# All scan drives on GpSimd, and the product placed behind both scans of the next pair

## The chip, the cores and the metric

The kernel runs on one core of one Trainium2 chip. The metric is the device time of one launch in microseconds (us): the median of 3 runs of the kernel before is 22461.38 us (22454.06 to 22490.8). The engines are called by the profile's names: PE (TensorE, matmuls), PEld (its weight loads), DVE (VectorE), ACT (ScalarE), POOL (GpSimd) and SP (SyncE, which issues most of the DMAs). Each engine runs its own list of instructions in order and waits on semaphores that the others raise.

## The reference, cut to what matters

The input is 64 samples of 96 channels by 28 x 28 pixels (784 pixels, in float32). Each sample passes through four layers; everything is computed per sample. The first layer is a convolution block (a 1x1 expansion to 576 channels, a 5x5 depthwise convolution with kernels mixed per sample, a squeeze gate, a 1x1 projection). The second is a group norm and a selective scan in four directions, the part that the change touches most:

```python
def step(h, inps):
    u_t, dt, B_t, C_t = inps
    dA = jnp.exp(dt[:, :, None] * A)
    h = dA * h + (dt * u_t)[:, :, None] * B_t[:, None, :]
    y = jnp.einsum('bdn,bn->bd', h, C_t) + Dv * u_t
    return (h, y)
```

It has 768 channels (4 directions of 192) with 16 states each, over 784 positions. The third layer mixes positions by a Fourier transform and adds a quantized two-layer network, the fourth is an attention without softmax (linear, so it folds into small matrices) and another such network.

## The kernel before

The 768 channels lie as six groups of 128 partitions. One **unit** is one group with one state index: 6 x 16 = 96 units per sample (`NU`), taken two by two as 48 **pairs** (`NP`, list `PAIRS`). A unit needs, in this order:

- a **decay**, exp(delta x A), 128x784, on ACT (`decaying`);
- a **drive**, (delta x u) x B, 128x784: in the even unit of a pair on DVE, in the odd one on POOL (`driving`, there are two functions of that name). The row of B comes broadcast to 128 partitions by DMA into one of four buffers `Bb`;
- a **scan** on DVE (`scanning`, the instruction TENSOR_TENSOR_SCAN): state = decay x state + drive along the 784 positions.

After both scans of a pair, PE sums halves of the partitions into PSUM (`state_sum`, the function `scan` of the tensor block: the "fold"). DVE multiplies that with C (`product`, into `prod`), and PE adds the products up in PSUM (`summation`, `scan_sum`).

The even unit's decay lies in PSUM (tile `decay_even`, one buffer), the odd unit's in SBUF (tile `decay`, two buffers). So the even scan reads one input from PSUM and one from SBUF, the odd scan reads both from SBUF. There are three state buffers and two drive buffers.

The scan of sample i is the backbone of a pass. Everything else is threaded between its units: the *tail* of sample i-1 (norm and gate behind the scan, `post`; the Fourier layer, `mixer`; the networks, `ffn`; `attention`), and the *head* of sample i+1 (the convolution layer, the group norm and the projections, `head` and `pre`). Each of these is a Python generator that yields a place on an axis counted in units (0 to 96); `go_on(between, 2 * p)` issues all steps whose place has come. The places are tables written out by hand: `CONV_SLOTS`, `HEAD`, `FAR`, `READ_AT`, `LOG_AT` and the numbers behind `yield`. They are the same for all engines, so a table sets the order on PE, ACT, DVE, POOL and SP at once. The loop (`Fori`) covers samples 1 to 62; samples 0 and 63 stand outside it.

For a DVE pair the order before is: drive of the even unit, even scan, product of the pair before, steps, odd scan, steps. POOL's list holds the odd drives, the twelve tiles of convolution weights per sample (`taps`) and one power (`gst`, reciprocal root of the group variance).

## Time and profile before

| | before |
|---|---|
| median of 3 runs | 22461.38 us |
| the profiled execution's own time | 22505.68 us |
| its span, first to last instruction | 22503.9 us |
| PE busy | 18818.0 us (84%) |
| DVE busy | 19251.1 us (86%) |
| ACT busy | 15624.5 us (69%) |
| POOL busy | 6356.1 us (28%) |
| mean granted TensorE clock | 0.894 |

Busy time is the sum of the time in which an engine executes instructions. Matmul ends are modelled, so a busy PE isn't a PE at its peak. Where a row gives "idle before" and a releaser, the engine stood still in front of that instruction until the one named had ended. An instruction that is held up after it has started shows no idle time: its own duration grows.

### The profile page before, as it was taken

Reading aid. Unit: us, or ns where it says so; the run is one execution under the profiler, and the core shown is the slowest. Engines: PE = TensorE matmul, PEld = TensorE weight load, DVE = VectorE, ACT = ScalarE, POOL = GpSimd, SP = SyncE. Lnnn points to the kernel's source line nnn. Section 1 sums busy time; section 2 is a strip of 40 time slices with the busy share of each in tenths; the row PEclk is TensorE's granted clock in tenths of the full one; section 3 lists DMA queues with packets and bytes.
Section 4 is the critical chain, followed back from the end, with each engine's and each line's share of the span. In section 5 each row is a group of like instructions: output and inputs, shape, how many; then the busy total and the mean of one; then the engine's idle time right before and its main releaser. Section 6 shows DMA issues by size and latency. Waiting matters only on the chain.

```text
span 22503.9 us, 334261 instructions
## 1 busy us (share of the span) xinstructions
PE 18818.0 (84%) x100834; PEld 6890.1 (31%) x100834; DVE 19251.1 (86%) x17938; ACT 15624.5 (69%) x21098; POOL 6356.1 (28%) x3909
## 2 busy tenths in 40 slices
PE   5888888888888888888888888888888888888887
PEld 1333333333333333333333333333333333333332
DVE  4888888888888888888888888888888888888887
ACT  3767777777677677776776777767767767777674
POOL 1222222222222222222222222222222222222222
PEclk8889898898898998988988889889889898898898
DMA  5555555555555555555555555545555555555552
GB/s 144 143 135 140 140 138 139 135 144 137 132 142 138 137 142 135 143 138 134 140 141 133 140 136 141 140 133 143 138 133 143 139 139 141 134 142 136 134 141 75
DMA packets 1418366, 3083.16 MB, mean 137 GB/s; under 512 B 207812, under 2 KB 786696, under 8 KB 1407859
## 3 DMA queue, kind: packets, MB, share of 16 engines
q1 hardware_dynamic: 1372146, 2992.85, 51.6%
q10 hardware_dynamic: 44032, 64.26, 1.1%
q8 instruction: 993, 16.27, 0.3%
q14 instruction: 1195, 9.78, 0.2%
HBM read 2796.25 MB, written 221.51 MB: 134 GB/s over the span
## 4 chain that ended last, share of the span: by engine, by line
issue 67%; POOL 15%; PE 8%; DVE 5%; ACT 4%; DMA 1%; POOLq 0%; ACTq 0%; SPq 0%; DVEq 0%
POOL drive L1576 13%; PE bank L575 3%; DVE state L1381 3%; PE state_sum L575 2%; PE pair L575 2%; POOL taps L1563 2%; ACT work L920 1%; DVE drive L1237 1%; PE scan_sum L575 1%; ACT L920 0%; ACT decay_even L920 0%; DVE work L1237 0%; ACT du L920 0%; DVE prod L1237 0%; ACT decay L920 0%
## 5 line engine op out<-in xcount | busy, mean ns | idle before, releaser
L1576 POOL TENSOR_TENSOR drive<-du,Bb 128x784 f32<-128x784 f32 x3072 | 5689.7, 1852 | 15638.6 <-DVE drive L1237 15638.6
L575 PE MATMUL state_sum<-state,fold 128*64 128x392 f32 x24576 | 5610.5, 585 | 1052.4 <-DVE state L1381 1029.9
L1381 DVE TENSOR_TENSOR_SCAN state<-decay_even,drive 128x784 f32<-128x784 f32 x3072 | 5500.2, 1790 | 128.4 <-ACT decay_even L920 17.6
L1381 DVE TENSOR_TENSOR_SCAN state<-decay,drive 128x784 f32<-128x784 f32 x3072 | 5473.3, 1782 | 0.2 <-POOL drive L1576 0.2
L920 ACT ACTIVATE decay_even<-delta,alog 128x784 f32<-128x784 f32 x3072 | 2821.6, 918 | 3240.8 <-DVE state L1381 3224.0
L1237 DVE TENSOR_TENSOR prod<-state_sum,Cb 128x784 f32<-128x784 f32 x3072 | 2950.6, 960 | 1906.4 <-PE state_sum L575 1902.4
L575 PE MATMUL scan_sum<-prod,fold 128*64 128x392 f32 x12288 | 2990.4, 568 | 1500.0 <-DVE prod L1237 1493.9
L575 PEld LDWEIGHTS state_sum<-state,fold 128*64 128x64 f32 x24576 | 1706.4, 154 | 4427.8 <-issue 2288.4
L575 PE MATMUL bank<-rep,taps 120*32 120x392 f32 x30720 | 2973.9, 514 | 96.1 <-ACT image L920 33.8
L920 ACT ACTIVATE decay<-delta,alog 128x784 f32<-128x784 f32 x3072 | 2890.3, 941 | 115.6 <-issue 72.7
L1237 DVE TENSOR_TENSOR drive<-du,Bb 128x784 f32<-128x784 f32 x3072 | 2943.0, 958 | 18.9 <-DVE work L1237 11.9
L914 ACT ACT_TABLE_LOAD x1707 | 2190.1, 1283 | 400.8 <-issue 375.3
L920 ACT ACT_TABLE_LOAD x1648 | 2114.4, 1283 | 33.6 <-DVE mean L1253 1.8
L575 PEld LDWEIGHTS scan_sum<-prod,fold 128*64 128x64 f32 x12288 | 660.1, 144 | 3173.8 <-DVE prod L1237 2436.7
L575 PEld LDWEIGHTS bank<-rep,taps 120*32 120x32 f32 x30720 | 856.1, 111 | 2175.3 <-issue 2022.2
L920 ACT ACTIVATE dwo<-bank,bn 128x392 f32<-128x392 f32 x768 | 521.1, 679 | 1402.0 <-PE bank L575 1401.9
L920 ACT ACTIVATE work<-pair 96x392 f32<-96x392 f32 (+5 forms) x2560 | 1135.7, 483 | 441.6 <-PE pair L575 421.4
L575 PE MATMUL bank<-dwo,wdl 6*128 6x392 f32 x1536 | 759.0, 575 | 401.9 <-ACT du L920 275.9
L575 PE MATMUL bank<-rep,wt 96*32 96x392 f32 x4608 | 518.8, 590 | 239.8 <-ACT xc L920 235.1
L920 ACT ACTIVATE work<-work 96x392 f32<-96x392 f32 (+6 forms) x897 | 492.4, 594 | 243.2 <-DVE work L1237 240.0
L920 ACT ACTIVATE work<-work,ffn_b 128x392 f16<-128x392 f16 (+1 forms) x1024 | 636.7, 622 | 33.4
L575 PE MATMUL pair<-work,mean 96*96 96x392 f32 (+1 forms) x1536 | 616.2, 524 | 22.2 <-ACT work L920 22.1
(169 smaller groups left out, 17504.8 us busy)
## 6 DMA issues: line engine op xcount, KB each, us to landing
Bb<-bc_rows SPq DMA_DIRECT2D x3072, 392.0 KB, 4.4
rep<-expanded_images SPq DMA_DIRECT2D x3840, 168.0 KB
Cb<-bc_rows SPq DMA_DIRECT2D x3072, 196.0 KB, 3.6
expanded_images<-image SPq DMA_DIRECT2D x1152, 112.0 KB, 2.5
rep<-conv_in_images SPq DMA_DIRECT2D x1152, 112.0 KB, 3.9
dwo<-in_pww SPq DMA_DIRECT2D x65, 1152.0 KB, 7.3
conv_in_images<-image SPq DMA_DIRECT2D x384, 112.0 KB, 3.2
xc<-xc ACTq DMA_DIRECT2D x384, 98.0 KB, 2.6
```

The lines of the kernel that those rows point to most:

```text
L575: return pe.matmul(out, lhsT, rhs, start=start, stop=stop)
L914: act.preload_act_table_set(LOG_EXP)
L920: return act.activation(out, in_, f, bias=bias, scale=scale, **more)
L1237: return v.tensor_tensor(out, a, b, op)
L1381: v.tensor_tensor_scan(state[:, j % STATES, :], DP[:, 0:L] if j % 2 == 0 else decay[:, j // 2 % DECAYS, :], drive[:, j % 2, :], 0.0, ALU.m ...
L1563: pool.tensor_tensor(taps[:, t % 2, cols, :], values.unsqueeze(2).to_broadcast([KP, n, 32]), cmask[:, :].unsqueeze(1).to_broadcast([KP, n, ...
L1576: pool.tensor_tensor(drive[:, j % 2, :], du[:, 2 * s + r, :], Bb[:, b % BSLOTS, :], ALU.mult).then_inc(drive_r.sem, 1)
```

## The change

Five things change; the computation stays the same.

1. POOL computes all 96 drives of a sample, DVE none. A drive waits until the scan two units earlier has ended (its buffer is free then).
2. On DVE the order for a pair is now: even scan, steps, odd scan, product of the pair before, steps.
3. There are three decay buffers used in turn, unit j taking number j mod 3. Number 0 lies in PSUM (tile `decay_third`), the others in SBUF. So of six units in a row, units 0 and 3 have their decay in PSUM and units 1, 2, 4 and 5 in SBUF. ACT issues the decay of unit j two units ahead of the place where its other steps stand. State buffers go from three to four; the space comes from `seT2`, which now lies in free partitions of `wdl`.
4. On PE the fold of a pair stands ahead of the summation of the pair before; it was behind it.
5. Steps of head and tail stand at other places; the power of the group norm moves from POOL to ACT (as Ln and Exp), and the bias of the squeeze gate is added by a matmul on PE where DVE added it.

```diff
-DECAYS = 2
+DECAYS = 3
 PRODS = 2
-STATES = 3
+STATES = 4
...
-CONV_SLOTS = (1, 2, 3, 5, 7, 8, 9, 10, 11, 12, 13, 14, 15, 17, 18, 19, 20, 21, 23, 24, 26)
+CONV_SLOTS = (1, 2, 3, 4, 6, 7, 9, 10, 11, 13, 14, 15, 16, 17, 18, 19, 20, 21, 23, 24, 26)
...
+        def decay_of(j):
+
+            return decay[:, j % DECAYS - 1, :] if j % DECAYS else DP[:, 0:L]
...
             def scan(i, *between):
                 for p in range(NP):
-                    if p >= 1:
-                        summation(i, p - 1)
-                    elif later(i):
-                        summation(i - 1, NP - 1)
-                    go_on(between, 2 * p + 1)
                     pe.wait_ge(state_r.sem, state_r.at(i, 2 * p + 2))
...
                     last.then_inc(folded.sem, 1)
                     go_on(between, 2 * p + 2)
+                    if p >= 1:
+                        summation(i, p - 1)
+                    elif later(i):
+                        summation(i - 1, NP - 1)
+                    go_on(between, 2 * p + 3)
...
+                if j >= DECAYS or later(i):
+                    act.wait_ge(state_r.sem, state_r.at(i, j - DECAYS + 1))
+                ac(decay_of(j), delta[:, k, :], ACT.Exp, scale=alog[:, k, n:n + 1]).then_inc(decay_r.sem, 1)
...
                 for p in range(NP):
-                    driving(2 * p)
                     scanning(2 * p)
+                    go_on(between, 2 * p)
+                    scanning(2 * p + 1)
                     if p >= 1:
                         product(i, p - 1)
                     elif later(i):
                         product(i - 1, NP - 1)
-                    go_on(between, 2 * p)
-                    scanning(2 * p + 1)
                     go_on(between, 2 * p + 1)
...
-                yield 64.4
-                pool.wait_ge(g_rs.sem, g_rs.at(i))
-                pool.tensor_tensor(gst[:, 6:7], gst[:, 6:7], eps[0:C, 2:3], ALU.pow).then_inc(g_pw.sem, 1)
...
-                pool.wait_ge(drive_r.sem, drive_r.at(i, j))
+                if j >= 2 or later(i):
+                    pool.wait_ge(state_r.sem, state_r.at(i, j - 1))
                 pool.tensor_tensor(drive[:, j % 2, :], du[:, 2 * s + r, :], Bb[:, b % BSLOTS, :], ALU.mult).then_inc(drive_r.sem, 1)
 
             def scan(i, *between):
-                for j in range(1, NU, 2):
+                for j in range(NU):
                     driving(i, j)
```

What it makes of the order is shown at three places of the loop's pass. (SCALAR_TENSOR_TENSOR with the output `state` is the scan; REGISTER_ALU and ISA rows compute the counts that are waited for.)

DVE at the first layer norm of the mixer (`work<-work 96x784`), before:

```order
L1381 SCALAR_TENSOR_TENSOR state<-decay,drive 128x784 [waits drive_ready]
L1417 ISA
L1419 TENSOR_TENSOR work<-work 96x784 [waits norm_rstd]
L1368 REGISTER_ALU
L1237 TENSOR_TENSOR drive<-du,Bb 128x784 [waits state_ready,b_loaded0]
L1377 REGISTER_ALU
L1380 REGISTER_ALU [waits even_decay]
L1381 SCALAR_TENSOR_TENSOR state<-decay_even,drive 128x784 [waits drive_ready]
L1237 TENSOR_TENSOR prod<-state_sum,Cb 128x784 [waits summed,states_folded,c_loaded1]
```

and after the change:

```order
L1376 SCALAR_TENSOR_TENSOR state<-decay_third,drive 128x784 [waits drive_ready,decay_ready]
L1368 REGISTER_ALU [waits c_loaded1]
L1249 TENSOR_TENSOR prod<-state_sum,Cb 128x784 [waits summed,states_folded]
L1411 ISA
L1413 TENSOR_TENSOR work<-work 96x784 [waits norm_rstd]
L1374 REGISTER_ALU
L1376 SCALAR_TENSOR_TENSOR state<-decay,drive 128x784 [waits drive_ready,decay_ready]
```

The drive is gone from DVE's list, the product stands behind the second scan of a pair, and the norm's multiplication stands behind the product where it stood behind a scan.

POOL at the beginning of a pass, before (odd drives, and `taps` of the next sample's convolution):

```order
L1574 ISA [waits b_loaded1]
L1575 ISA [waits du_ready]
L1576 TENSOR_TENSOR drive<-du,Bb 128x784 [waits drive_ready]
L1574 REGISTER_ALU [waits b_loaded1]
L1575 REGISTER_ALU [waits du_ready]
L1576 TENSOR_TENSOR drive<-du,Bb 128x784 [waits drive_ready]
L1558 ISA
L1563 TENSOR_TENSOR taps<-kern,cmask 120x320 [waits bank_read]
```

and after:

```order
L1567 ISA [waits b_loaded0]
L1569 ISA [waits du_ready]
L1570 TENSOR_TENSOR drive<-du,Bb 128x784 [waits state_ready]
L1570 TENSOR_TENSOR drive<-du,Bb 128x784 [waits state_ready,du_ready,b_loaded1]
L1567 REGISTER_ALU [waits b_loaded0]
L1569 REGISTER_ALU [waits du_ready]
L1570 TENSOR_TENSOR drive<-du,Bb 128x784 [waits state_ready]
L1569 REGISTER_ALU [waits du_ready,b_loaded1]
L1570 TENSOR_TENSOR drive<-du,Bb 128x784 [waits state_ready]
L1554 ISA
L1559 TENSOR_TENSOR taps<-kern,cmask 120x320 [waits bank_read]
```

Two drives per pair stand in POOL's list now, and each waits for a scan (`state_ready`) where it waited for DVE's drive.

PE around the squeeze gate of the next sample (`bank<-zse`) and the last matmuls of the mixer (`w2T`), before:

```order
L575 MATMUL pair<-cosm,work 96x396 x2
L719 REGISTER_ALU
L575 MATMUL scan_sum<-prod,fold 64x392 x2
L638 REGISTER_ALU
L575 MATMUL bank<-zse,seT 128x1 x6
L699 REGISTER_ALU
L575 MATMUL state_sum<-state,fold 64x392 x4
L575 MATMUL pair<-work,w2T 96x392 x4
```

and after:

```order
L577 MATMUL state_sum<-state,fold 64x392 x4
L640 REGISTER_ALU
L577 MATMUL bank<-seb,ident 128x6
L577 MATMUL bank<-zse,wdl 128x1 x6
L577 MATMUL scan_sum<-prod,fold 64x392 x2
L577 MATMUL pair<-work,w2T 96x392 x4
```

The fold (`state_sum`) of a pair now precedes the summation (`scan_sum`) of the pair before, and one small matmul brings the gate's bias.

## Rows read from the trace of the kernel before

**Rows 1.** The page's span and busy times (engine, us, share, instructions)
```profile
span 22503.9 us, 334261 instructions
PE 18818.0 (84%) x100834; PEld 6890.1 (31%) x100834; DVE 19251.1 (86%) x17938; ACT 15624.5 (69%) x21098; POOL 6356.1 (28%) x3909
```
**Rows 2.** The scans by tile: duration ns min/median/max, first and last start
```profile
L1381 DVE TENSOR_TENSOR_SCAN state<-decay_even,drive x3072: 1790/1790/1793, 343.0 to 22363.5; 128x784 f32<-128x784 f32 x192
L1381 DVE TENSOR_TENSOR_SCAN state<-decay,drive x3072: 1775/1781/2028, 345.0 to 22366.1; 128x784 f32<-128x784 f32 x192
```
**Rows 3.** DVE groups by form (busy us, mean ns, idle before, releaser)
```profile
L1237 DVE TENSOR_TENSOR prod<-state_sum,Cb 128x784 f32<-128x784 f32 x3072 | 2950.6, 960 | 1906.4 <-PE state_sum L575 1902.4 <-issue 0.8
L1237 DVE TENSOR_TENSOR drive<-du,Bb 128x784 f32<-128x784 f32 x3072 | 2943.0, 958 | 18.9 <-DVE work L1237 11.9 <-issue 4.4
L1237 DVE TENSOR_TENSOR du<-delta,xc 128x784 f32<-128x784 f32 x384 | 374.7, 976 | 41.0 <-DVE delta L1237 0.5
...
L1237 DVE TENSOR_TENSOR pwm<-pwm,sc 128x576 f32<-128x576 f32 x64 | 47.7, 745 | 0.3 <-ACT sc L920 0.3
```
**Rows 4.** DVE's waits: waited for, us in total, times, longest
```profile
DVE prod L1237 <- PE state_sum L575: 1902.4, 1265, 6.1
DVE work L1237 <- PE pair L575: 483.3, 171, 5.7
...
DVE state L1381 <- ACT decay_even L920: 17.6, 49, 2.5
```
**Rows 5.** POOL groups by form
```profile
L1576 POOL TENSOR_TENSOR drive<-du,Bb 128x784 f32<-128x784 f32 x3072 | 5689.7, 1852 | 15638.6 <-DVE drive L1237 15638.6
L1563 POOL TENSOR_TENSOR taps<-kern,cmask 120x320 f32<-120x320 f32 x768 | 556.7, 725 | 224.2 <-ACT pwm L920 160.8 <-PE bank L575 63.4
```
**Rows 6.** One ordinary pair in order of time (start, us): DVE
```profile
10003.41 0.95 DVE L1237 TENSOR_TENSOR drive<-du,Bb 128x784 f32<-128x784 f32 x1
10004.39 1.79 DVE L1381 TENSOR_TENSOR_SCAN state<-decay_even,drive 128x784 f32<-128x784 f32 x1
10006.71 0.97 DVE L1237 TENSOR_TENSOR prod<-state_sum,Cb 128x784 f32<-128x784 f32 x1 [0.52 <-PE state_sum L575]
10007.60 1.78 DVE L1381 TENSOR_TENSOR_SCAN state<-decay,drive 128x784 f32<-128x784 f32 x1
```
**Rows 7.** The same pair: POOL
```profile
10004.44 1.86 POOL L1576 TENSOR_TENSOR drive<-du,Bb 128x784 f32<-128x784 f32 x1 [4.53 <-DVE drive L1237]
```
**Rows 8.** The power on POOL, all 64: duration ns min/median/max
```profile
L1567 POOL TENSOR_TENSOR gst<-gst,eps x64: 550/2222/2224, 282.8 to 21940.3; 96x1 f32<-96x1 f32 x64
```
**Rows 9.** One of the 64 in order of time: POOL, and the scan beside it
```profile
11584.29 2.22 POOL L1567 TENSOR_TENSOR gst<-gst,eps 96x1 f32<-96x1 f32 x1 [1.55 <-DVE gst L1341]
...
11584.16 1.79 DVE L1381 TENSOR_TENSOR_SCAN state<-decay,drive 128x784 f32<-128x784 f32 x1
```
**Rows 10.** The longest SBUF scan, and POOL beside it, in order of time
```profile
422.64 0.95 DVE L1237 TENSOR_TENSOR prod<-state_sum,Cb 128x784 f32<-128x784 f32 x1
423.50 2.03 DVE L1381 TENSOR_TENSOR_SCAN state<-decay,drive 128x784 f32<-128x784 f32 x1
...
423.16 0.73 POOL L1563 TENSOR_TENSOR taps<-kern,cmask 120x320 f32<-120x320 f32 x1
```
**Rows 11.** Busy us per engine from first to last scan (counts in brackets)
```profile
343.00:22367.90 22024.90, 18611.51 (x99818) 6799.36 (x99818) 19136.94 (x17774) 15525.97 (x20917) 6346.05 (x3891) 0.90 0.53 138
```
**Rows 12.** PE's waits on DVE: us in total, times, longest
```profile
PE scan_sum L575 <- DVE prod L1237: 1493.9, 886, 5.0
PE state_sum L575 <- DVE state L1381: 1029.9, 883, 13.8
```
**Rows 13.** From the page: ACT's decays and table loads, and the B loads
```profile
L920 ACT ACTIVATE decay_even<-delta,alog 128x784 f32<-128x784 f32 x3072 | 2821.6, 918 | 3240.8 <-DVE state L1381 3224.0
...
L914 ACT ACT_TABLE_LOAD x1707 | 2190.1, 1283 | 400.8 <-issue 375.3
...
Bb<-bc_rows SPq DMA_DIRECT2D x3072, 392.0 KB, 4.4
```

More of the change, by code:

```diff
@@ L50 @@
 SETUP_LINKS = 51
-LEAD_LINKS = 5
+LEAD_LINKS = 4
 TAIL_LINKS = 2
@@ L98 @@
-FAR = {("delta", m, h): slot(k) + SECOND * h for m, k in ((2, 4), (3, 6), (4, 16), (5, 22)) for h in range(2)}
+HEAD.update({("hidden",): 53.1, ("gate",): 55.1, ("point", 0): 58.1, ("point", 1): 60.3, ("group",): 63.1,
+             ("proj", 0): 67.1, ("proj", 1): 69.1, ("proj", 2): 71.1, ("conv3", 0): 73.1, ("conv3", 1): 75.1, ("conv3", 2): 77.1,
+             ("dbl",): 81.1, ("delta", 0, 0): 84.3, ("delta", 0, 1): 85.1, ("delta", 1, 0): 87.1, ("delta", 1, 1): 89.1,
+             ("mix", 0): 91.1, ("mix", 1): 93.1})
@@ L177, in build @@
         S = ps("state_sum", 1024)
-        DP = ps("decay_even", 1024)
+        DP = ps("decay_third", 1024)
         TT = ps("pair", 1024)
```

211 lines of the change are left out of this document (100 added, 111 removed).

## The prediction

> **What bounds the kernel now.** I read the page's busy times first, then where DVE stands still, then which instructions of DVE and POOL run beside each other and which don't.
>
> DVE is busy for 86% of the span, PE for 84%, POOL for 28% [rows 1]. The scans fill the launch: the first starts at 343.0, the last at 22366.1 and ends 1.78 later, so a sample takes (22367.9 - 343.0) / 64 = 344.1 us. The 479 us outside them (set-up and first head, last tail) hold few of the changed instructions and count as unchanged [rows 2]. Of a sample's 344.1 us DVE is busy 19136.9 / 64 = 299.0, PE 290.8, ACT 242.6, POOL 99.2 [rows 11]. So DVE bounds, with 45 us of waits a sample: 29.8 of them in front of products, for PE's fold [rows 3, 4].
>
> The change takes 48 drives of 958 ns from DVE, 46.0 us a sample [rows 3], and puts 48 drives of 1852 ns on POOL [rows 5]. By busy times alone DVE falls to 253 us and POOL rises to 188, both far below 344. What speaks against reading it so is how POOL and DVE share SBUF:
>
> - An odd drive on POOL runs beside the even scan and costs neither anything: 1.86 us beside a scan of 1.79, as in every pair [rows 6, 7]. That scan reads its decay from PSUM; its minimum and maximum over 3072 are 1790 and 1793 ns [rows 2].
> - The power on POOL takes 550 ns once, in sample 0, with no scan beside it, and 2222 at the median [rows 8]. In the case shown [rows 9] the SBUF scan starts at 11584.16 and ends at 11585.95, POOL starts at 11584.29 and ends at 11586.51: 0.56 after the scan's end. POOL stood still for the rest of the scan and then ran its full time: the hand-over costs 0.01.
> - The other way round there is one case. The longest SBUF scan, 2028 ns against a median of 1781 [rows 2], started at 423.50 while POOL's `taps` ran from 423.16 to 423.89, and ended at 425.53 [rows 10]: 1.64 us after POOL's end. So the scan was held off too, but it had started up meanwhile: behind POOL it costs 1.64, which is 0.14 less than 1.78.
>
> So a DVE instruction with both inputs in SBUF and a POOL instruction exclude each other. Before, the order kept them apart: every POOL drive lies under a PSUM scan. After, four of six scans read SBUF, and there are twice as many POOL drives. The bound of the new kernel is what DVE and POOL must do one after the other.
>
> **The change part by part.** Per sample, what excludes each other:
>
> - 64 SBUF scans of 1.781 [rows 2]: 114.0 us.
> - 96 drives of 1.852 [rows 5]: 177.8.
> - 12 `taps` of 0.725 [rows 5]: 8.7.
> - Thirteen DVE groups with two SBUF inputs besides the drives, from `du` (374.7 us) to `pwm` (47.7) [rows 3], 1973 us together: 30.8.
>
> Sum: 331.3 us. PSUM scans (32 x 1.790) and products (48 x 0.960, one input from PSUM) run beside POOL and lie underneath. Written out for six units with scans P S, S P, S S (P reads PSUM): scan 0 runs 0 to 1.79 beside drive 1; drive 2 follows at 1.85 and holds scan 1 off until 3.70; scan 1 ends at 5.49; drive 3 runs beside a product and holds scan 2 off until 7.34; scan 2 ends at 9.12; scan 3 runs beside drive 4 until 10.97; drive 5 holds scan 4 off until 12.83; scans 4 and 5 end at 16.4; drive 6 ends at 18.25, where scan 6 begins as scan 0 did. The cycle is 4 x 1.781 + 6 x 1.852 = 18.24 us with one of the two always at work, 6.08 per pair; each product is hidden with about 0.9 us to spare.
>
> Hand-overs, from the same cycle, 16 cycles a sample. Three scans in six start behind a drive: 48 x -0.14 = -6.7 us. One drive starts behind a scan that began first: 16 x 0.01 = 0.2. Two drives start on a scan's signal, with 0.08 us between the DVE drive's end at 10004.36 and POOL's start at 10004.44 [rows 6, 7]: 32 x 0.08 = 2.6. Together -3.9. For the scan behind a drive there is one row only; as the other end I take the signalled start's +0.08, that is -6.7 and +3.8 us a sample; the value is that of the scan's own row.
>
> Waits of DVE that stay. Today the fold may start at the odd scan's end, and the product follows a drive and a scan later, 2.75 us. Now the fold may start at the end of the product before (that frees `state_sum`), and its own product stands two scans later, 3.6 us at the least and, in a pair of 6.9, six. PE's lateness thus has 0.8 to 3.2 us more room. The waits average 1.5 us, the longest is 6.1 [rows 4]; I keep 4 of the 29.8. Where DVE waits in tail steps (483.3 us for `pair`, 171 times [rows 4]: 7.6 a sample), POOL still has one or two drives to run, 1.85 to 3.7 us, against a mean wait of 2.8; I keep 2. Estimate: 6 us, ends 0 and 23 (half of the product waits and all of the `pair` waits).
>
> Costed at nothing: ACT gets 6 table loads more per pass (70 rows for 64) of 1.283 us, 7.7 a sample, and the power; ACT is idle for 101 us of 344, 3224 us of it waiting for scans [rows 11, 13]. Without that cover it is 7.7 us. Three decays in turn let ACT run two scans ahead; waits for decays are 17.6 us in all today [rows 4]. SP now waits for POOL's drives before it reloads `Bb`; behind that wait stand the C rows and the image rows. A buffer is needed again six units later, some 20 us, and a load lands in 4.4 [rows 13]. The gate's extra matmul and the smaller DVE steps are tenths of a microsecond a sample. The moved steps of tail and head keep their instructions and DMAs and shift by a pair or so; I count them in the waits.
>
> T = 331.3 - 3.9 + 6 = 333.4 us a sample, 10.7 less than 344.1: 685 us over 64. The profiled execution (22505.7) would be 21,821; the median shown lies 44 below it, so 21,780.
>
> **The rivals.**
>
> *PE takes the bound (slower).* PE has 290.8 us of work a sample and stands idle 53, of which (1493.9 + 1029.9) / 64 = 39.4 wait for DVE's products and scans [rows 11, 12]. The fold used to start at the odd scan's end; now a product of 0.96 lies between, since it frees `state_sum`. In the 883 folds that waited for a scan [rows 12] PE would start 0.96 later: 848 us. For it: PE's idle is 15% only, and it works in order, so time lost in front of a fold is lost for all that stands behind. Against it: the summation no longer waits, its product being done. It decides when PE's idle stays above 333.4 - 290.8 = 43 us a sample; if all 53 stay and the 848 come on top it gives 22,461 + 848 = 23,310, if a third of the 848 comes 22,740.
>
> *Hand-overs cost where I let them give (no change).* If each of the 64 blocked starts a sample (48 scans, 16 drives) costs as much as a start on a signal, 0.08 us [rows 6, 7], the hand-overs are 5.1 + 2.6 = 7.7 in place of -3.9 and T = 331.3 + 7.7 + 6 = 345.0: 22,520. For it: 48 of the 64 rest on a single row. Against it: that row and the 62 or so long powers [rows 8, 10]. With waits of 5 instead of 6, or 0.07 instead of 0.08, it is no change.
>
> The Trainium skill (SBUF — State Buffer, sections "SBUF: two separate sides" and "A bandwidth-pool intuition that's wrong (but worth ruling out)") calls the shared ports an exclusive lock that the first to start keeps for its whole instruction, and puts the blocked one's resumption at the holder's end plus about 115 ns. On the exclusion the trace agrees (2222 against 550 ns, 2028 against 1781); on the 115 ns it shows +0.01 and -0.14 us. By 115 ns (an estimate from that page) the 64 starts would cost 7.4 us a sample and this rival's time would be 22,660.
>
> *All waits are hidden and every blocked DVE step gains (faster still).* T = 331.3 - 3.9 - 37 x 0.14 = 322.2, if the 37 instructions of the thirteen groups start behind a drive too and save what a scan saves: 21,060.
>
> *The change doesn't do what it says:* DVE's and POOL's order show that it does, and the exclusion is in the rows; a sharing of the ports that began only after the start, with DVE's 253 and PE's 291 us as the bounds, has the power's standstill of 1.66 us against it. Under it PE's 291 and a third of its idle, 309, give 20,200.
>
> **How the numbers follow.** Forecast (T from 326 to 342): 0.58, its own range 21,300 to 22,350. PE as the bound: 0.20. Costly hand-overs: 0.10. Faster still: 0.08. Sharing: 0.04. About 0.2%, 45 us, is what a measurement of this kernel can tell from no change. Of the hand-over case 0.03 fall to faster, 0.05 within and 0.02 to slower. Faster 0.58 + 0.08 + 0.04 + 0.03 = 0.73, slower 0.20 + 0.02 = 0.22, same 0.05. The range reaches from 20,900, short of the sharing case, to 22,900, where the waits' upper end (T = 350.4, 22,860) and the milder part of the PE case lie.
>
> **What would show it.** Right: POOL drives with a mean well above 1.85 or SBUF scans well above 1.78, since standstill shows as duration; `decay_third` scans still at 1.790; idle before products far below 1906 us; DVE and POOL busy together above the 331 us a sample. Wrong: drives and scans at their old means, which is sharing; idle before products near or above 1906 us with PE's idle unchanged, which is the PE case; waits of scans for decays in hundreds of us, which would put ACT in place of POOL.

## The result

The changed kernel takes 23,411.5 us (median; 23,333.6 to 23,424.4) against 22,467.8 for the kernel before measured beside it: 1.0412 times as long, 95% interval 1.0387 to 1.0437. The prediction was 21,780 us, range 20,900 to 22,900, 0.73 for faster. It is wrong in sign and outside the range.

The page's span and busy times of the changed kernel, as in [rows 1]:

```profile
span 23419.2 us, 336875 instructions
PE 18984.1 (81%) x100962; PEld 7007.4 (30%) x100962; DVE 19561.5 (84%) x14739; ACT 16298.7 (70%) x21663; POOL 14387.7 (61%) x6917
```

DVE has 3199 instructions fewer and is busy longer than before, 19,561.5 us against 19,251.1. The scans by tile (duration minimum/median/maximum in ns, first to last start), as in [rows 2], say why:

```profile
L1376 DVE TENSOR_TENSOR_SCAN state<-decay,drive x4096: 1755/1791/3476, 346.4 to 23280.3; 128x784 f32<-128x784 f32 x196
L1376 DVE TENSOR_TENSOR_SCAN state<-decay_third,drive x2048: 1753/1776/1793, 344.7 to 23274.4; 128x784 f32<-128x784 f32 x187
```

The PSUM scans never exceed 1793 ns; the SBUF scans reach 3476, which is 1.7 us, most of a drive, above their median. A sample takes (23280.3 + 1.79 - 344.7) / 64 = 358.4 us, against 344.1 before and 333.4 predicted. The groups of DVE and POOL in the changed kernel (busy us, mean ns, idle before, releaser), as in [rows 3, 5]:

```profile
L1376 DVE TENSOR_TENSOR_SCAN state<-decay,drive 128x784 f32<-128x784 f32 x4096 | 9299.8, 2280 | 646.5 <-POOL drive L1570 394.5 <-ACT t L924 220.8 <-DVE t L1249 11.8
L1376 DVE TENSOR_TENSOR_SCAN state<-decay_third,drive 128x784 f32<-128x784 f32 x2048 | 3636.3, 1776 | 401.1 <-POOL drive L1570 340.5 <-ACT decay_third L924 41.1 <-issue 15.3
L1249 DVE TENSOR_TENSOR prod<-state_sum,Cb 128x784 f32<-128x784 f32 x3072 | 2909.2, 947 | 498.6 <-PE state_sum L577 493.0 <-issue 4.7
L1475 DVE CAST work<-work 128x392 fp8e5<-128x392 f16 x768 | 546.5, 712 | 102.0 <-ACT work L924 101.8
L1249 DVE TENSOR_TENSOR du<-delta,xc 128x784 f32<-128x784 f32 x384 | 476.8, 1242 | 40.0
...
L1570 POOL TENSOR_TENSOR drive<-du,Bb 128x784 f32<-128x784 f32 x6144 | 13084.8, 2141 | 8445.1 <-DVE state L1376 8309.9 <-DVE du L1249 100.7 <-DMA Bb<-bc_rows 2.9
L1559 POOL TENSOR_TENSOR taps<-kern,cmask 120x320 f32<-120x320 f32 x768 | 1350.4, 1759 | 444.8 <-PE bank L577 285.0 <-ACT pwm L924 159.4
```

Standstill counts as duration. Of the 2943 us of drives taken from DVE [rows 3], the SBUF scans alone give back 4096 x (2280 - 1781) ns = 2044 us. The thirteen other two-input groups grew too, by 979 us together (`du` from 976 to 1242 ns), and the casts of L1475 by 277 (352 to 712 ns). That is more than the drives took away. The product's idle is down from 1906.4 us to 498.6, as forecast. But DVE's idle as a whole (span less busy) is up from 3252.8 us to 3857.7: apart from the products it went from 1346.4 to 3359.1. Where it went is in DVE's waits (waited for: us in total, times, longest), as in [rows 4]:

```profile
DVE state L1376 <- POOL drive L1570: 735.0, 769, 2.1
DVE work L1495 <- PE pair L577: 642.7, 188, 11.2
DVE work L1413 <- ACT work L924: 532.4, 256, 13.3
DVE prod L1249 <- PE state_sum L577: 493.0, 290, 6.8
```

L1495 are three of the five small steps of the tail's attention (the other two wait for 1.4 us in all), L1413 the norms' multiplications. Waits of DVE's `work` for `pair`, over all its lines, were 528.6 us in before (483.3 of them in [rows 4], the two other attention steps included) and are 949.0 now (642.7 + 176.6 + 129.7); the norms' line waited 33.9 us in before, 5 times. The five attention steps alone waited 467.1 us in before and 644.1 now.

From the first to the last scan, as in [rows 11] (us; busy time of PE, PEld, DVE, ACT, POOL):

```profile
344.70:23282.10 22937.40, 18770.23 (x99939) 6912.55 (x99939) 19446.22 (x14576) 16198.50 (x21478) 14373.34 (x6898) 0.88 0.49 132
```

Of a sample's 358.4 us DVE stands idle for 54.5, PE for 65.1 and ACT for 105.3.

**One account for all runs.** The prediction's sum was a time of exclusive work plus what remains. The same two terms can be taken from any trace, over all rows from the first scan of sample 2 to that of sample 62: *U*, the time in which POOL or a DVE instruction with two SBUF inputs stands in the trace (overlaps once; the tiny `gst` steps are left out), and *N*, the rest, in which neither does. N is not all waiting: DVE's other work (scans and products with an input from PSUM, casts, copies) counts there while POOL stands still. The period of a sample is U + N. Predicted were U = 331.3 - 3.9 = 327.4 and N = 6. Measured in the changed kernel: U = 318.5, N = 41.4. (In us per sample; this period, 359.9, leaves out the first and last samples.)

| run | ratio to before | U | N | period |
|---|---|---|---|---|
| before | 1 | 255.5 | 89.7 | 345.3 |
| the change | 1.0412 | 318.5 | 41.4 | 359.9 |
| e4_before_all_pool | 1.0453 | 296.3 | 65.7 | 361.9 |
| e2_split_drives | 1.1070 | 279.3 | 103.6 | 383.0 |
| e3_split_even_psum | 1.0202 | 256.6 | 97.4 | 354.0 |
| e6_even_psum | 1.0128 | 291.5 | 59.1 | 350.6 |
| e1_all_psum | 1.0017 | 213.9 | 132.7 | 346.6 |
| e8_before_pool_psum | 1.0149 | 214.2 | 136.7 | 350.9 |
| e5_conv_three_taps | 1.0286 | 318.3 | 36.9 | 355.2 |
| e5b_psum_three_taps | 0.9961 | 213.5 | 130.8 | 344.2 |
| e7_three_drives | 1.0358 | 316.7 | 41.8 | 358.6 |
| e10_no_attention_wait | 1.0254 | 318.4 | 36.8 | 355.2 |
| e10b_psum_no_attention_wait | 0.9886 | 213.8 | 128.2 | 342.0 |
| e9b_late_product_only | 1.0619 | 256.9 | 110.1 | 367.0 |
| e11_images_sooner | 1.0308 | 318.4 | 37.4 | 355.8 |
| e12_even_psum_images_sooner | 1.0084 | 291.4 | 56.0 | 347.4 |

Of the 41.4 us DVE is at work in 24.4 and stands idle in 17.1. The parts: 14.7 are PSUM scans beside which POOL has no drive to run, 9.0 waits of DVE's steps for `pair`, 3.1 products, 3.1 waits of `work` for `work`; the rest is spread over a dozen other steps.

### The profile page after: what moved, and what is told of

Read it like the earlier page. It is cut to its first block, busy times and chain, and to the rows that moved or that the text cites. A ratio compares the mean times of both kernels' runs of the same rounds, so it can differ in the third digit from the quotient of the medians.

```text
span 23419.2 us, 336875 instructions
## 1 busy us (share of the span) xinstructions
PE 18984.1 (81%) x100962; PEld 7007.4 (30%) x100962; DVE 19561.5 (84%) x14739; ACT 16298.7 (70%) x21663; POOL 14387.7 (61%) x6917
## 4 chain that ended last, share of the span: by engine, by line
issue 27%; PE 22%; POOL 17%; ACT 12%; DVE 8%; DMA 8%; SPq 5%; ACTq 0%; DVEq 0%; POOLq 0%
POOL drive L1570 16%; PE bank L577 10%; PE pair L577 5%; PE state_sum L577 5%; DVE state L1376 4%; DMA rep<-expanded_images 4%; ACT work L924 3%; DMA rep<-conv_in_images 2%; ACT L924 2%; PE scan_sum L577 2%; ACT L918 2%; ACT du L924 2%; DVE prod L1249 1%; SPq L530 1%; POOL taps L1559 1%
## 5 line engine op out<-in xcount | busy, mean ns | idle before, releaser
L1570 POOL TENSOR_TENSOR drive<-du,Bb 128x784 f32<-128x784 f32 x6144 | 13084.8, 2141 | 8445.1 <-DVE state L1376 8309.9
L1376 DVE TENSOR_TENSOR_SCAN state<-decay,drive 128x784 f32<-128x784 f32 x4096 | 9299.8, 2280 | 646.5 <-POOL drive L1570 394.5
L577 PE MATMUL state_sum<-state,fold 128*64 128x392 f32 x24576 | 5593.7, 583 | 2526.2 <-DVE prod L1249 2516.6
L924 ACT ACTIVATE decay<-delta,alog 128x784 f32<-128x784 f32 x4096 | 3859.9, 946 | 2932.7 <-DVE state L1376 2875.7
L1376 DVE TENSOR_TENSOR_SCAN state<-decay_third,drive 128x784 f32<-128x784 f32 x2048 | 3636.3, 1776 | 401.1 <-POOL drive L1570 340.5
L577 PE MATMUL bank<-rep,taps 120*32 120x392 f32 x30720 | 3057.9, 525 | 371.9 <-DMA rep<-expanded_images 221.1
L1249 DVE TENSOR_TENSOR prod<-state_sum,Cb 128x784 f32<-128x784 f32 x3072 | 2909.2, 947 | 498.6 <-PE state_sum L577 493.0
L924 ACT ACTIVATE decay_third<-delta,alog 128x784 f32<-128x784 f32 x2048 | 1871.6, 914 | 866.0 <-DVE state L1376 792.3
L924 ACT ACT_TABLE_LOAD x1834 | 2353.0, 1283 | 34.4 <-DVE mean L1265 1.8
L1559 POOL TENSOR_TENSOR taps<-kern,cmask 120x320 f32<-120x320 f32 x768 | 1350.4, 1759 | 444.8 <-PE bank L577 285.0
L577 PE MATMUL pair<-work,mean 96*96 96x392 f32 (+1 forms) x1536 | 676.6, 569 | 106.0 <-ACT work L924 106.0
L1413 DVE TENSOR_TENSOR work<-work 96x784 f32<-96x784 f32 (+1 forms) x256 | 311.9, 1218 | 532.4 <-ACT work L924 532.4
L1249 DVE TENSOR_TENSOR delta<-delta,du 128x784 f32<-128x784 f32 x384 | 581.2, 1514 | 144.4 <-ACT du L924 144.4
```

Source lines behind the costliest of these rows:

```text
L577: return pe.matmul(out, lhsT, rhs, start=start, stop=stop)
L924: return act.activation(out, in_, f, bias=bias, scale=scale, **more)
L1249: return v.tensor_tensor(out, a, b, op)
L1376: v.tensor_tensor_scan(state[:, j % STATES, :], decay_of(j), drive[:, j % 2, :], 0.0, ALU.mult, ALU.add).then_inc(state_r.sem, 1)
L1413: v.tensor_tensor(out, w[0][0:C, :], w[1][0:C, :], ALU.mult, **more).then_inc(ln_r.sem, 1)
L1559: pool.tensor_tensor(taps[:, t % 2, cols, :], values.unsqueeze(2).to_broadcast([KP, n, 32]), cmask[:, :].unsqueeze(1).to_broadcast([KP, n, ...
```

## The experiments

### How much the exclusion costs

`e4_before_all_pool` is the kernel before with every drive on POOL and nothing else changed:

```diff
-                    driving(2 * p)
...
-                for j in range(1, NU, 2):
+                for j in range(NU):
```

> The kernel before with the first part alone done: all drives on POOL, each waiting for the scan two units earlier; everything else as before. Theory 1: exclusive work is 48 SBUF scans 85.5 + 96 POOL drives 177.8 + 8.7 + 30.8 = 303 us; with 25 to 50 us in which neither works 328 to 353 us a sample, 21,400 to 23,000. Theory 2, which puts the loss on the order of product and fold: DVE is relieved of 46 us and nothing else changes, 20,500 or less.

Measured: 23,532.2 us, 1.0453 (1.0436 to 1.0471), outside both theories. Taking the drives from DVE makes the kernel slower by itself, in the old order and at the old places. Its SBUF scans are held off, 2227 ns in place of 1782, while the PSUM scans take 1770:

```profile
L1381 DVE TENSOR_TENSOR_SCAN state<-decay,drive 128x784 f32<-128x784 f32 x3072 | 6839.9, 2227 | 0.1
L1381 DVE TENSOR_TENSOR_SCAN state<-decay_even,drive 128x784 f32<-128x784 f32 x3072 | 5438.4, 1770 | 334.2 <-POOL drive L1576 316.2 <-DVE work L1237 13.0 <-ACT decay_even L920 3.8
```

These durations show the exclusion; the slower time by itself does not, since the old order with the drives on POOL stays slower than before without excluding scans too (e8 below). The time is above what theory 1's sum gave: U is 296.3, near its 303, but N is 65.7 and not 25 to 50.

`e1_all_psum` is the changed kernel with no scan that reads two SBUF inputs. There is no room in PSUM for two whole decays, so only half a decay is computed and its first column is read for all:

```diff
-            return decay[:, j % DECAYS - 1, :] if j % DECAYS else DP[:, 0:L]
+            return DP[:, 512 * (j % 2):512 * (j % 2) + HALF]
...
-                    v.tensor_tensor_scan(state[:, j % STATES, :], decay_of(j), drive[:, j % 2, :], 0.0,
+                    v.tensor_tensor_scan(state[:, j % STATES, :], decay_of(j)[:, 0:1].to_broadcast([128, L]), drive[:, j % 2, :], 0.0,
```

> The changed kernel, but every scan reads its decay from PSUM, so that no scan excludes a POOL drive. Each decay is computed over 392 of the 784 columns into one of two PSUM banks, and the scan reads its first column for all positions; order, drives and waits for scans stay, a decay may run two units ahead instead of three. Theory 1 (exclusion of SBUF scans and POOL drives costs the time): POOL drives fall from a mean of 2.14 us to 1.85-1.95, scans stay at 1.78-1.79, and a sample falls from 360 us towards DVE's own 253 plus its waits, 295 to 315 us: 19,300 to 20,600 us. Theory 2 (PE starts its folds later because the product now stands in front of them, and PE is the bound): PE's work is the same, so 22,700 us or more.

Measured: 22,540.2 us, 1.0017 (1.0004 to 1.0029) to before, 0.962 (0.960 to 0.965) to the changed kernel. Scans and drives in its trace:

```profile
L1377 DVE TENSOR_TENSOR_SCAN state<-decay_third,drive 128x784 f32<-128x784 f32 x6144 | 10826.4, 1777 | 1593.7 <-ACT decay_third L924 970.5 <-ACT t L924 558.0 <-issue 35.7
L1571 POOL TENSOR_TENSOR drive<-du,Bb 128x784 f32<-128x784 f32 x6144 | 11569.5, 1891 | 9758.1 <-DVE state L1377 9488.8 <-DMA Bb<-bc_rows 144.7 <-DVE du L1250 99.7
```

Scans at 1777 and drives at 1891 ns run beside each other; the exclusion of scans is gone. This edit takes 871 us off the 23,411. But 104.6 us of U a sample went and N took back 91.3. Most of that is bookkeeping: 85.5 us of this run's N are scans beside which POOL has no drive to run (14.7 in the change); DVE spends its 1.78 us on each as before. With DVE busy for 17,486.9 us only, the kernel is still no faster than before. So a second limit stands just under the first, and theory 1, which let the gain through, fails; theory 2's 22,700 is missed as well.

The run is not a clean removal, so 871 us is not the price of the exclusion alone. It halves ACT's work for the decays. With two decays in turn in place of three, scans wait 970.5 us for them, against 41.1 in the change. And only scans are freed: the thirteen other two-input groups of DVE still take 910 us more than in before, and the casts 322.

`e2_split_drives` puts the even drives back on DVE and leaves all else of the change.

> The changed kernel with the first part alone undone: DVE computes the even drives again, POOL the odd ones, which wait for DVE's drive. Product order, buffers and places stay. Theory 1: exclusive work a sample is 48 POOL drives 88.9 + 64 SBUF scans 114 + 48 DVE drives 46 + taps 8.7 + other DVE steps 30.8 = 288 us; DVE is the bound again with 299 us and fewer product waits than before, 325 to 340 us a sample: 21,200 to 22,200. Theory 2: the order of fold and product is unchanged, so it stays at 23,000 or more.

Measured: 24,920.4 us, 1.1070 (1.1052 to 1.1089), the slowest of all. Its SBUF scans:

```profile
L1386 DVE TENSOR_TENSOR_SCAN state<-decay,drive 128x784 f32<-128x784 f32 x4096 | 10727.1, 2628 | 545.6 <-ACT t L924 210.0 <-POOL drive L1580 61.1 <-DVE t L1249 11.8
```

With decays in turns of three, POOL's odd drives fall on scans that read SBUF, and with DVE's drives beside them DVE is busy for 22,705.5 us (91%). The time lies in theory 2's range, but what grew is the scans, which theory 2 did not name. The decays' turn and the drives' place belong together; what keeps POOL's drives under PSUM scans is the old turn (in e3, the next run, SBUF scans take 1842 ns).

`e3_split_even_psum` adds the old turn to e2, so that only the order of product and fold, the fourth state, the new places and the moved small steps (the group norm's power, the gate's bias) remain of the change:

```diff
-            return decay[:, j % DECAYS - 1, :] if j % DECAYS else DP[:, 0:L]
+            return decay[:, j // 2 % 2, :] if j % 2 else DP[:, 0:L]
```

> As the run with split drives, and the decays as in the kernel before (all even units in PSUM, the odd ones in two SBUF buffers), so that every POOL drive can lie under a PSUM scan; on ACT the steps of a place stand ahead of an even decay. What remains of the change is the product behind both scans, the fold ahead of the summation, four states and the new places. Theory 1: 320 to 335 us a sample, 20,900 to 21,900. Theory 2: 23,000 or more.

Measured: 22,971.9 us, 1.0202 (1.0185 to 1.0219), far above theory 1 and just under theory 2. That part costs 2% by itself while DVE still has its drives.

`e6_even_psum` is e3 with all drives on POOL, that is, the changed kernel with the old turn of the decays. (ACT's steps of a place then stand ahead of an even decay, as in e3, and ACT loads its tables 372 times less often.)

> The changed kernel with every even decay in PSUM and the odd ones in two SBUF buffers (48 instead of 64 scans of a sample read two SBUF inputs; the kernel's output is the reference's). Theory 1 (it is the number of excluding scans that costs): a quarter of the 870 us that the run with one-port scans took off, so 23,150 to 23,250 us. Theory 2 (with two drive buffers POOL is out of work beside a PSUM scan, so that a PSUM scan more is uncovered time): 23,350 to 23,700 us, with POOL's idle for state above 8,310 us.

Measured: 22,804.4 us, 1.0128 (1.0108 to 1.0147). Both theories miss: more comes back than a quarter of 871 us. Its scans and drives:

```profile
L1379 DVE TENSOR_TENSOR_SCAN state<-decay,drive 128x784 f32<-128x784 f32 x3072 | 6303.5, 2052 | 444.3 <-ACT t L924 422.8 <-DVE t L1252 11.8
L1379 DVE TENSOR_TENSOR_SCAN state<-decay_third,drive 128x784 f32<-128x784 f32 x3072 | 5476.3, 1783 | 979.4 <-POOL drive L1573 790.7 <-ACT decay_third L924 163.2 <-DVE work L1252 11.8
L1573 POOL TENSOR_TENSOR drive<-du,Bb 128x784 f32<-128x784 f32 x6144 | 13941.8, 2280 | 7775.7 <-DVE state L1379 7624.2 <-DVE du L1252 104.4 <-DMA Bb<-bc_rows 9.2
```

16 SBUF scans fewer a sample are 28.5 us; U fell by 27.0 and N rose by 17.7, so a third arrives. The rise is PSUM scans beside which POOL has no drive: 34.4 us in place of 14.7. From e6 to e1 another 48 go and a twentieth arrives. The exclusion is what binds at the top, and each step down meets more of the second limit.

These runs lead from before to the change in three steps: before 22,496 (beside e3); order, states, places and small steps +476 (e3); drives to POOL -168 (e6); decays in turns of three, with ACT's order that goes with them, +607 (the change). Sum +915 (944 against the 22,467.8 measured beside the change). As ratios, the drives' step is 0.993 (0.990 to 0.995) and the decays' 1.028 (1.025 to 1.031), from the ratios to before with their half-widths added in quadrature. So in the new order the drives' move did gain: 168 us, a quarter of the 685 that the prediction gave the whole.

The size of a step depends on what was changed before it. Taken the other way round, the drives' move in the old order costs 1037 us (e4), and order, states, places and small steps then take 728 off (e4 to e6). The two parts are worth something only together, and no single price belongs to either. The third step is the same on both ways. Its 607 us hold the decays' turn and ACT's order; that the 372 table loads are the cost is unlikely, as e1 has them all and is faster than e6, but the two were not tried apart.

### The order, and TensorE

`e8_before_pool_psum` gives the old order and the old places the relief of e1:

```diff
-                    decaying(j, DP[:, 0:L], 2, even_r)
+                    decaying(j, DP[:, 0:HALF], 2, even_r)
...
-                    decaying(j, decay[:, j // 2 % DECAYS, :], 2 * DECAYS, odd_r)
+                    decaying(j, DP[:, 512:512 + HALF], 2, odd_r)
```

> The kernel before, in its old order and with its old places of the head's and tail's steps, with all 96 drives of a sample on POOL and every decay in PSUM (shortened to 392 columns and broadcast), so that scans and drives do not exclude each other: the same relief as the run with one-port scans, but none of the rest of the change. Theory 1 (the change's order of the product, the fold and its places cost time by themselves, some 2% as the run with split drives and even decays in PSUM says): 21,800 to 22,200 us. Theory 2 (the order costs nothing, and the lack of a gain without exclusion lies in ACT's and TensorE's steps, which are the same in both): 22,400 to 22,700 us, as the run with one-port scans.

Measured: 22,836.6 us, 1.0149 (1.0130 to 1.0169). Both theories miss, theory 1 on the wrong side: with POOL at the drives the new order is 296 us better than the old (e1), and with excluding scans 728 (e6 against e4). In e8 DVE stands idle in front of products again (its longest group of waits; here the profile names no releaser):

```profile
DVE prod L1237 <- issue: 3366.8, 1546, 8.1
```

So the new order costs with drives on DVE and pays with drives on POOL.

`e9b_late_product_only` is the kernel before with each product behind both scans of the next pair and four states, TensorE's order untouched:

```diff
                     scanning(2 * p)
+                    go_on(between, 2 * p)
+                    scanning(2 * p + 1)
                     if p >= 1:
                         product(i, p - 1)
...
-                    go_on(between, 2 * p)
-                    scanning(2 * p + 1)
```

> The kernel before with one part of the change alone: each product stands behind both scans of the next pair, with four state buffers; drives, decays, places and TensorE's order as before (the output is the reference's). Theory 1 (DVE's waits before products, 1,906 us in before, go): 21,900 to 22,250 us. Theory 2 (they turn into waits at the steps of tail and head, as in the run with split drives and even decays in PSUM): 22,400 to 22,700 us.

Measured: 23,885.4 us, 1.0619 (1.0602 to 1.0637): outside both theories. TensorE's list has the summation of a pair, and a place's steps, ahead of the next fold. PE's wait for products in front of the summation, 1493.9 us in before [rows 12], is now

```profile
PE scan_sum L575 <- DVE prod L1237: 3986.2, 1547, 7.2
```

and what stands behind it in TensorE's list comes later. e3, with the swap on TensorE and the new places, is 913 us faster. That the swap is what makes the late product bearable is likely, but not shown: it was not tried without the new places.

`e5_conv_three_taps` and `e5b_psum_three_taps` take work from TensorE, in the changed kernel and in e1:

```diff
-                for dx, wait in enumerate((0.0, 0.3, 0.6, 1.2, 1.5)):
+                for dx, wait in enumerate((0.0, 0.3, 0.6)):
```

> The changed kernel with two of the five dx of every 5x5 convolution left out (that part of the convolution is not computed): TensorE has some 19 us a sample, about 1,200 us in all, less to do; DVE, POOL and ACT do the same as before. Theory 1 (the exclusion of scans and drives and the two drive buffers set the time, TensorE is beside the path): within 0.7% of the changed kernel, 23,250 to 23,500 us. Theory 2 (what is left of DVE's waiting is for TensorE in the steps that lie between the scans): 22,200 to 22,900 us, with the wait of the projection casts for the bank 'pair' well under 640 us.

> The run with one-port scans (every scan reads a decay in PSUM, whose decay is shortened to 392 columns and broadcast, so scans and drives do not exclude each other) with two of the five dx of every 5x5 convolution left out as well. Theory 1 (with the exclusion gone the time is set by POOL's or DVE's own work and hand-overs): as without the shorter convolution, 22,400 to 22,650 us. Theory 2 (with the exclusion gone TensorE's steps are the bound, in the order of the changed kernel): 21,300 to 22,000 us, more taken off than the same edit takes off the changed kernel.

Measured: 23,143.7 us, 0.988 (0.985 to 0.991) of the changed kernel, and 22,408.2 us, 0.994 (0.993 to 0.996) of e1. PE's busy time fell by 1049 us (18,984.1 to 17,935.1), the time by 268: between the two theories. TensorE is not the bound, though some of its work lies on the path. In e1 132 us come off, which is at the lower edge of theory 1, so the amount of TensorE's work is not the second limit either.

### What the time without exclusive work is made of

`e7_three_drives` lets POOL run three units ahead:

```diff
-        drive = sb("drive", [128, 2, L])
+        drive = sb("drive", [128, 3, L])
...
-                if j >= 2 or later(i):
-                    pool.wait_ge(state_r.sem, state_r.at(i, j - 1))
+                if j >= 3 or later(i):
+                    pool.wait_ge(state_r.sem, state_r.at(i, j - 2))
```

> The changed kernel with three drive buffers in place of two (room made by one transform table standing in for another, so that part of the computation has other values). Theory 1 (with two drive buffers POOL is out of work beside a PSUM scan, 14.7 us a sample in which neither POOL nor a DVE instruction with two SBUF inputs runs): some 10 us a sample come back, 22,650 to 22,900 us, and POOL's idle for state falls. Theory 2 (DVE's waits for TensorE and ACT in the steps between the scans make up the rest, and POOL only gets ahead and then waits): 23,250 to 23,450 us.

Measured: 23,318.1 us, 0.995 (0.992 to 0.998) of the changed kernel. POOL's idle for `state` fell from 8309.9 to 6494.3 us, N stayed at 41.8. Theory 2 holds: a buffer more takes 93 us off and is no cure. PSUM scans without a drive still make 13.7 us of N.

`e10_no_attention_wait` and `e10b_psum_no_attention_wait` let the five attention steps wait for nothing:

```diff
-                    v.wait_ge(sm_mm.sem, sm_mm.at(i, n + 1))
-                    src = T[n % 2][0:rows, 0:cols]
+                    src = ident[0:rows, 0:cols]
```

> The changed kernel in which DVE's five small attention steps of the tail (places 77 to 81) copy a constant in place of TensorE's results and so wait for nothing (the attention's matrices are left out). They are 643 us of DVE's waiting and the longest pair of a sample, 12.6 us against 5.3. Theory 1 (what the prediction left out is DVE's waiting in the steps between the scans, on top of the exclusive work): 8 to 9 us a sample in which neither POOL nor DVE's two-input instructions run go, 22,800 to 22,950 us. Theory 2 (POOL and DVE are behind for the exclusive work alone, and a wait taken away at one place comes back at the next): 23,250 to 23,450 us.

> The run with one-port scans (every scan reads a short PSUM decay) with the five attention steps waiting for nothing as well (the attention's matrices are left out). The pair at that place took 14.4 us, 9.7 of them waiting. Theory 1 (without the exclusion the time is the sum of DVE's work and its waits at the steps, and the order of the steps is what holds the kernel there): 21,850 to 22,100 us. Theory 2 (another bound, TensorE or ACT as a whole, stands just below): 22,350 to 22,550 us.

Measured: 23,084.1 us, 0.985 (0.982 to 0.988) of the changed kernel; 22,246.5 us, 0.987 (0.985 to 0.989) of e1. Both lie between the theories. Of 643 us of waits 327 came off, of 849 us 294. Much of the rest turned up at the next products: DVE's wait for `state_sum` grew from 493.0 to 792.8 us in the one and from 565.1 to 939.4 in the other. So these waits are on the path, and about half of one that goes is found again. The pair at that place, 39, is the longest of a sample with 12.6 us (the mean is 7.5); in the kernel before it took 10.7 already, so only part of its wait is the change's.

What makes one of them can be read in the trace of the changed kernel. The chain that leads to pair 39 of sample 20 (start us, us, what; SPq is the issuing on SP's queue):

```profile
7797.33 0.88 DVE prod L1249
7798.21 0.45 SPq L461
...
7800.10 0.36 SPq L453
...
7800.65 0.34 SPq L530
...
7803.63 7.29 DMA rep<-conv_in_images
...
7810.97 4.15 PE bank L577 x24
7815.12 0.58 PE pair L577 x2
7815.72 0.06 DVE work L1495
```

A product frees the C rows' buffer; SP reloads it (L461), then the B rows (L453), and only then issues the image of the third 3x3 convolution (L530). That lands 7.3 us after its last issue; the convolution runs on PE, and the attention's small matmul is queued behind it. TensorE's matmuls of the same convolution (idle before in brackets), for the second image and for the third:

```profile
7800.91 2.23 PE L577 MATMUL bank<-rep,wt 96*32 96x392 f32 x24 [1.11 <-ACT xc L924]
...
7810.97 4.15 PE L577 MATMUL bank<-rep,wt 96*32 96x392 f32 x24 [4.34 <-DMA rep<-conv_in_images]
```

and the stretches of time around it (us; busy time and count of PE, PEld, DVE, ACT, POOL; granted clock, DMA share, GB/s):

```profile
7797.50:7803.00 5.50, 3.63 (x32) 1.18 (x32) 5.50 (x4) 4.23 (x5) 3.78 (x3) 1.00 0.76 203
...
7810.90:7815.10 4.20, 4.13 (x25) 1.03 (x25) 0.00 (x0) 0.08 (x1) 0.00 (x0) 0.50 0.73 190
```

For 4.2 us DVE and POOL both do nothing, while a convolution runs at a granted clock of 0.50 (1.2 GHz) after PE had idled 4.34 us; the same 24 matmuls took 2.23 us at 1.00 (2.4 GHz). `e11_images_sooner` takes this chain apart: the three projection steps go back to their old places, on every engine, and the third image's load stands ahead of the B and C rows.

```diff
-("proj", 0): 67.1, ("proj", 1): 69.1, ("proj", 2): 71.1,
+("proj", 0): 67.1, ("proj", 1): 68.3, ("proj", 2): 69.1,
...
-AT["conv3", s - 2] + 1.6 if s >= 2 else 0.0)
+AT["conv3", s - 2] + 0.4 if s >= 2 else 0.0)
```

> The changed kernel with the three projection steps of the head at the places of the kernel before (67.1, 68.3, 69.1, read at 68.5, 69.0, 70.5) and the load of the third convolution image 1.2 places sooner, so that on SP it stands ahead of the loads of B and C rows that wait for a drive and a product (the output is the reference's). Theory 1 (the longest wait, the attention step at pair 39, is the end of a chain: product, C rows on SP, the third image's load of 7.3 us, the 3x3 convolution on TensorE and behind it the attention's small matmul, and the change's places made it): 3 to 5 us a sample go, 23,050 to 23,250 us, with DVE's wait of work for pair well under 640 us. Theory 2 (the wait has another last cause, or comes back at once at the next step): 23,330 to 23,450 us.

Measured: 23,183.1 us, 0.990 (0.987 to 0.993) of the changed kernel. The waits in its trace:

```profile
DVE work L1495 <- PE pair L577: 404.8, 164, 5.2
```

Theory 1 holds: 228 us come back by the places of three steps and the order of a few loads (the two were not tried apart), the longest of these waits is 5.2 in place of 11.2 us, and pair 39 takes 8.4 in place of 12.6 us (means over samples 2 to 61). N fell by 4.0, U did not move.

`e12_even_psum_images_sooner` has the same edits in e6.

> The same three places and the same sooner load in the changed kernel with every even decay in PSUM (the output is the reference's): the best of what the runs point to that still computes the reference. Theory 1: both gains add, 607 us for the decays and 200 to 300 us for the chain: 22,500 to 22,650 us, level with the kernel before or just above it. Theory 2 (they do not add): 22,750 to 22,850 us.

Measured: 22,669.4 us, 1.0084 (1.0059 to 1.0110) to before, 0.996 (0.993 to 0.999) of e6: 135 us, where the same edits took 228 off the change; the time lies between the theories, just above the first. The run computes what the reference computes and recovers 742 us of the change, but is still slower than the kernel before. Of the runs that compute the whole, none is faster than the kernel before.

## Why the prediction was wrong

- **The exclusion and its price: right.** SBUF scans and drives wait for each other, PSUM scans do not, and U came out at 318.5 for 327.4 predicted, 3% below. A scan's start behind a drive costs what its single row said. In the changed kernel at 7630 us (start, us):

```profile
7630.09 2.81 DVE L1376 TENSOR_TENSOR_SCAN state<-decay,drive 128x784 f32<-128x784 f32 x1
...
7629.39 1.87 POOL L1570 TENSOR_TENSOR drive<-du,Bb 128x784 f32<-128x784 f32 x1 [3.69 <-DVE state L1376]
```

  The drive ends at 7631.26 and the scan at 7632.90, 1.64 us later, as in [rows 10]. Of all 1827 SBUF scans that began while POOL was at work the median is 1.65 us, and none lies outside 1.64 to 1.66; they are 28.5 a sample, where I had counted 48. The other way round the price was wrong, to the kernel's favour: the 950 drives that began under a scan end 1.66 us behind it, 0.19 less than a free drive takes, where I had put +0.01 from the power's row. So the rivals of costly hand-overs and of shared ports fall (the SBUF scans of e4 speak against the second too), and the one in which all waits are hidden falls with N.
- **The step that failed: "Waits of DVE that stay ... Estimate: 6 us, ends 0 and 23", and with it the six-unit cycle "with one of the two always at work".** Both together stand for N, and N measured 41.4. The larger part, 24.4 us, is a term that I had put at nothing ("run beside POOL and lie underneath"): DVE at work outside the exclusive sum while POOL stands still, 14.7 of it PSUM scans without a drive beside them. The cycle holds only while nothing else is in DVE's list. The other 17.1 us are uncovered waits of DVE, for 6 predicted: inside my ends, but nearly three times the value. The waits were taken over from before, where DVE's steps came late enough for their inputs. From the first to the last scan DVE's idle rose from 45.1 to 54.5 us a sample. The product's part shrank from 29.8 to 498.6 / 64 = 7.8, near the 4 that I kept; the rest grew from 15.3 to 46.7. Part of that is the exclusion itself (735.0 us of scans waiting for drives), and POOL is at work in most of it.
- **"A buffer is needed again six units later, some 20 us, and a load lands in 4.4": failed in what stands behind it.** I named the image rows behind the B and C rows on SP's queue and costed them at nothing. The chain above runs through just that place, and e11 got 228 us back there. (The run also moved three steps back.) Image loads (`rep<-conv_in_images`) land in 5.5 us at the median in the changed kernel, in 4.0 in e11 and in 3.9 in before.
- **"The moved steps ... I count them in the waits": not a price that stands alone.** Together with the order of product and fold they cost 476 us with the drives on DVE (e3), but with the drives on POOL, as in the change, they take 728 off (e4 to e6). How that divides between order and places is open, but for the one chain.
- **The three decays: weighed in one direction only.** Their 16 additional SBUF scans were in the sum, but I never set against them a version with the old turn. Going back to it, with ACT's steps ahead of the even decay, takes off 607 us, nearly two thirds of the loss (e6).
- **The rival of TensorE: the time, not the mechanism.** Its 23,310 us lies near the result. But its price, later folds, is not there: PE waits for DVE's products 2516.6 us in front of folds, and in before 1493.9 + 1029.9 = 2523.8 at both places [rows 12]. And with 1049 us less for PE the time fell by 268 (e5). The sign that I gave the rival, more than 43 us of PE's idle a sample, is there (65.1), but it would be there whatever holds a sample at 358 us, so it decides nothing.
- **"ACT is idle for 101 us": held.** It is 105.3 in the changed kernel. Waits of scans for the decays themselves stayed small (41.1 us for `decay_third`). The 220.8 us that stand with ACT's `t` are not among them: in all 91 cases the scan's own decay had ended 1.9 us or more before. They stand at unit 13 (63 times) and unit 85 (28 times), behind the places where the mixer and the second network wait for such a copy.

What the second limit is, at 22,250 to 22,550 us with no scan excluded, stays open. It is neither TensorE's amount of work (e5b) nor the attention's wait alone (e10b). What is left in e1 is DVE's list, with 1232 us of standstill still in its other two-input steps and casts, its waits at steps whose inputs come over several engines in a fixed order, and the waits for decays that the edit itself made; no run takes these apart.

## What to carry to other kernels

A sum of exclusive work gives a floor, not a time: ask in which stretches neither side has work, and do not take DVE's waits for the steps between as small as today's places make them. Count as well the work of either side that excludes nothing but finds the other out of work. When an engine is relieved in a kernel with a fixed order, look at what stands behind each new wait in the queues, the loading queue above all, and follow it to the next step of the relieved engine. Split a change of several parts into a chain of kernels, each with one part more, and walk it in a second order too: here the drives' move gained 168 us behind the new order and cost 1037 in front of it.

## What the runs showed of the hardware

- A cast with one SBUF input and an SBUF output is held off by POOL as well. In the kernel before, 768 of them took 352 ns each:

```profile
L1481 DVE CAST work<-work 128x392 fp8e5<-128x392 f16 x768 | 259.9, 352 | 131.7 <-ACT work L920 130.2
```

  In the changed kernel they take 712, and in e1, where no scan excludes POOL, 771. In the changed kernel the 395 that began while a drive ran took 1359 ns at the median, and none with no POOL instruction beside it took over 367. That is 277 us in all which the sum of thirteen two-input groups did not hold. The Trainium skill (SBUF — State Buffer, section "Who interferes with whom") lists casts among the operations that can enter a mode in which they contend with GpSimd; the trace agrees by these durations.
- POOL's `taps`, two SBUF inputs as well, went from 725 to 1759 ns. Standstill falls on whichever starts second: in the changed kernel on 1827 scans that began under POOL and on 950 drives that began under a scan. The second one's start-up overlaps with the block: a scan ends 1.65 us behind the drive (1.78 by itself), a drive 1.66 us behind the scan (1.85 by itself).
- TensorE's granted clock fell to 0.50 in a stretch that followed an idle time of 4.34 us, and a convolution of 24 matmuls took 4.15 instead of 2.23 us: a late load is paid for twice.
